# A message-passing GNN on one core: pairs of groups and a deeper ring in the two sums, one signal fewer in the two maxima

## The chip, the core and the metric

One NeuronCore of a Trainium2 chip runs the whole program. TensorE (PE) multiplies into PSUM, VectorE (DVE) and ScalarE (ACT) read PSUM, GpSimd (POOL) issues indirect DMAs that gather rows, SyncE (SP) issues plain DMAs. The engines wait for each other through semaphores, counters that an instruction raises when it is done. The metric is the device time of one execution in microseconds (us); lower is better.

## The reference

There are 12500 nodes with 96 features and 200000 edges sorted by destination. Four rounds pass over all the edges:

```
h  = relu(layernorm(x))
n1 = mean over edges of h[src];   n2 = mean over edges of n1[src]
x  = x + 0.5 * n1 + 0.5 * n2                      # rounds 0 and 1: sums
h  = relu(layernorm(x))
c1 = leaky(max over edges of (h[src] @ W1_msg + edge_attr @ W1_edge) + h @ W1_root + b1)
c2 = leaky(max over edges of (c1[src] @ W2_msg + edge_attr @ W2_edge) + c1 @ W2_root + b2)
out = x + c2                                      # rounds 2 and 3: maxima
```

A node without edges gets 0. All is float32; the inputs are drawn at random.

## The kernel before

The edges are cut into batches of 128, one edge a partition, and four batches make a group: 391 groups, 1564 batches. Each round has an edge phase (all groups) and a node phase (14 chunks of seven tiles of 128 nodes), and a table in HBM holds the values that the round gathers from. The phases of a round follow each other; the change touches the edge phases alone.

*Gather (all rounds).* GpSimd runs a stream written out in full: for each group four indirect DMAs (L374), each 128 rows of 384 bytes into one slot of a ring `rows` of `RING` = 8 groups. Before a group from the ninth on it waits until the group that had the slot is used: for `picked` in the sums, for `rows_ps` in the maxima, both raised by TensorE.

*Sums (rounds 0 and 1).* In a batch the edges of one node are neighbours. VectorE builds for each group four one-hot matrices from the edge's rank within its batch's window (`hots`, L767; L773 in round 0 builds a second set for counting the nodes of each tile), two groups ahead. TensorE (`sum_windows`) multiplies each batch's rows by its one-hot (L557, four matmuls of two records each) into one of two PSUM banks (`WIN + j % 2 * BANK`), raises `picked`, and in round 0 multiplies ones by the counting one-hots (L563), raising `counted`. It starts a group when the rows have landed, the one-hots are there and the fold two groups back is done. VectorE's `fold` (L784) waits for `picked`, loads four start positions into registers and adds four windows into `comp`, one after another. In round 0 ScalarE writes a column of node numbers into each ring slot (`stage_ids`, L435).

*Maxima (rounds 2 and 3).* TensorE's order within a step g is: `rows_of(g)` (edge features times weights, L576, and the rows by identity, L578; raises `rows_ps`), `back(g-1)` (transposes the running maxima, L589; raises `runT_ps`), `pick(g-2)` (one-hots pick the last of each segment, L600; raises `picked`). VectorE scans each group (L799) and builds its one-hots; ScalarE copies the transposes to SBUF (`copy_running`, L443) and the picked windows into `comp` (`windows`, L452).

`sweeps` runs a body of eight groups: once written out, then in a loop, then the rest. VectorE, ScalarE and TensorE use it; GpSimd's stream has no loop. Waits are in each engine's program order; nothing is reordered.

## Time and profile before

| | us |
|---|---|
| median of 3 runs | 9666.22 |
| lowest, highest | 9662.51, 9667.9 |
| the profiled execution | 9629.93 |
| its span, first to last instruction | 9628.2 |
| GpSimd busy | 6458.6 (67%) |
| TensorE busy | 5576.1 (58%) |
| VectorE busy | 3262.5 (34%) |
| ScalarE busy | 1500.7 (16%) |

The profile is one execution, recorded by the hardware. "Idle before" is the time an engine did nothing before an instruction, and the arrow names what ended it: "issue" is nothing that the profile shows, "remote" a semaphore update whose origin it does not show. The granted clock of TensorE has two levels, 0.5 (1.2 GHz) and 1.0 (2.4 GHz). Matmul ends are modelled. Round 0's edge phase is about 60 to 2331 us, round 1's 2412 to 4666, round 2's 4776 to 7113, round 3's 7212 to 9550.

### The profile page before, as it was taken

The page shows a single profiled execution, that of the slowest core. Times are in us where ns is not written, and L with a number is a line of the kernel's source. Part 1 is how long each engine was busy: PE and PEld are TensorE (multiplying, and loading weights), DVE is VectorE, ACT ScalarE, POOL GpSimd, SP SyncE. Part 2 cuts the span into 40 slices and gives each one's busy share as a digit, 9 for nine tenths or more (in the row PEclk, how much of TensorE's full clock was granted, in tenths as well). Part 3 has the DMA queues.
Part 4 walks back from the last instruction along what each step waited for, and adds up shares of the span by engine and source line. Part 5 has one row for each costly group of instructions (what it writes and reads, how often), then busy time and mean ns, then how long its engine had stood idle before and what let it go on. Part 6 is the DMA issues. An engine that isn't in the chain of part 4 may idle for free.

```text
span 9628.2 us, 100471 instructions
## 1 busy us (share of the span) xinstructions
PE 5576.1 (58%) x25651; PEld 4095.6 (43%) x25651; DVE 3262.5 (34%) x6693; ACT 1500.7 (16%) x5073; POOL 6458.6 (67%) x6525
## 2 busy tenths in 40 slices
PE   2333333334233333333578877878887887887888
PEld 1222222223222222222555555555564555555556
DVE  4333333334333232323423333333332333333334
ACT  1000000001000000000322222222232222222223
POOL 5666666664666666666566666766656666666665
PEclk6555555556555555555767777777786777677776
DMA  3111111111111111111133333333323333333332
GB/s 79 35 34 34 34 34 34 34 35 39 47 35 34 34 34 35 34 34 35 46 76 77 77 77 77 78 80 78 77 64 71 80 78 77 77 77 77 77 81 64
DMA packets 309643, 548.56 MB, mean 57 GB/s; under 512 B 183464, under 2 KB 183464, under 8 KB 284712
## 3 DMA queue, kind: packets, MB, share of 16 engines
q0 software_dynamic: 200192, 307.90, 16.3%
q1 hardware_dynamic: 108804, 239.50, 9.7%
q14 instruction: 77, 0.63, 0.0%
q8 instruction: 22, 0.36, 0.0%
q10 hardware_dynamic: 548, 0.17, 0.0%
HBM read 522.27 MB, written 24.87 MB: 57 GB/s over the span
## 4 chain that ended last, share of the span: by engine, by line
another core or an unknown queue 29%; PE 26%; issue 9%; DVE 8%; DVEq 2%; ACT 1%; ACTq 1%; POOL 0%; DMA 0%; POOLq 0%; SPq 0%
PE ps L578 7%; PE ps L576 6%; PE ps L600 6%; PE ps L589 3%; DVE arena L799 3%; DVE comp L784 3%; PE ps L557 2%; DVE arena L767 2%; DVEq L257 1%; DVEq L784 1%; PE ps L662 1%; PE ps L638 0%; ACTq L257 0%; PE ps L675 0%
## 5 line engine op out<-in xcount | busy, mean ns | idle before, releaser
L374 POOL DMA_INDIRECT rows<-table,src_sb x6256 | 6273.4, 1003 | 2930.3 <-issue 1767.5
L557 PE MATMUL ps<-arena,rows 128*98 128x128 f32 (+1 forms) x6256 | 1418.1, 399 | 2967.0 <-DVE comp L784 2634.6
L557 PEld LDWEIGHTS ps<-arena,rows 128*98 128x98 f32 (+1 forms) x6256 | 1179.5, 254 | 3226.7 <-DVE comp L784 2836.3
L799 DVE TENSOR_TENSOR_SCAN arena<-arena,ps 96x512 f32<-96x512 f32 x782 | 996.6, 1274 | 3238.6 <-remote 1989.8
L784 DVE TENSOR_TENSOR comp<-comp,ps 98x128 f32 (+1 forms) x3128 | 893.6, 286 | 2878.4 <-remote 2317.0
L578 PEld LDWEIGHTS ps<-ident,rows 128*96 128x96 f32 x6256 | 950.4, 208 | 912.9 <-issue 912.7
L600 PE MATMUL ps<-arena 128*96 128x128 f32 x6256 | 1180.2, 352 | 108.6 <-issue 72.4
L578 PE MATMUL ps<-ident,rows 128*96 128x128 f32 x6256 | 1173.3, 344 | 54.2 <-issue 53.4
L576 PE MATMUL ps<-arena,we 32*96 32x512 f32 x1564 | 1143.7, 819 | 27.3 <-DMA rows<-table,src_sb 27.3
L600 PEld LDWEIGHTS ps<-arena 128*96 128x96 f32 x6256 | 1052.2, 228 | 129.6 <-issue 124.4
L767 DVE TENSOR_TENSOR arena<-iota_b,meta 128x512 f32<-128x512 bf16 x1564 | 1053.0, 673 | 59.6 <-issue 55.1
L452 ACT COPY comp<-ps 96x128 f32 x3128 | 821.3, 263 | 1490.8 <-PE ps L600 573.6
L589 PE MATMUL ps<-ident,arena 96*128 96x96 f32 x3128 | 564.2, 322 | 757.8 <-DVE arena L799 653.8
L589 PEld LDWEIGHTS ps<-ident,arena 96*128 96x128 f32 x3128 | 449.1, 190 | 831.0 <-DVE arena L799 657.9
L443 ACT COPY arena<-ps 128x384 f32<-128x384 f32 x782 | 374.5, 479 | 1998.1 <-remote 1233.2
L435 ACT COPY rows<-root 128x4 f32 (+1 forms) x391 | 74.3, 197 | 2179.0 <-remote 1581.1
L492 ACT COPY rel_c<-node_rel 128x7 f32<-128x7 f32 (+1 forms) x42 | 8.5, 203 | 2261.8 <-DVE comp L784 2261.8
L388 POOL TENSOR_SCALAR arena<-iota,rel_c 128x128 f32<-128x128 f32 x252 | 172.0, 698 | 228.4 <-ACT rel_c L492 134.0
L576 PEld LDWEIGHTS ps<-arena,we 32*96 32x96 f32 x1564 | 236.2, 196 | 186.9 <-issue 125.4
L773 DVE TENSOR_TENSOR arena<-iota_b,meta 128x392 bf16<-128x392 bf16 x391 | 219.5, 561 | 12.0 <-issue 11.6
L563 PE MATMUL ps<-arena,ones_b 128*1 128x392 bf16 x391 | 168.3, 430 | 0.0
L662 PE MATMUL ps<-arena 128*128 128x96 f32 (+1 forms) x784 | 141.1, 354 | 6.4 <-ACT arena L504 4.8
(84 smaller groups left out, 1026.0 us busy)
## 6 DMA issues: line engine op xcount, KB each, us to landing
arena<-flags SPq DMA_DIRECT2D x194, 768.0 KB
rows<-table,src_sb POOLq DMA_INDIRECT x6256
arena<-in_eat SPq DMA_DIRECT2D x194, 256.0 KB
table<-arena SPq DMA_DIRECT2D x56, 336.0 KB, 2.7
out<-xs SPq DMA_DIRECT2D x13, 336.0 KB
xs<-in_x SPq DMA_DIRECT2D x6, 672.0 KB, 5.9
arena<-flags SPq DMA_DIRECT2D x2, 576.0 KB
src_sb<-in_srcs SPq DMA_DIRECT2D x1, 782.0 KB, 5.2
```

Source lines behind the costliest of these rows:

```text
L374: pool.indirect_dma_start(rows[:, g % RING, j, 0:D], None, tables[r][:, :], bass.IndirectOffsetOnAxis(src_sb[:, c:c + 1], 0)).then_inc(lan ...
L443: act.copy(runT[:, slot % SCANS].rearrange("p k d -> p (k d)"), ps[:, RUNT + slot % 2 * BANK:RUNT + slot % 2 * BANK + GRP * D]).then_inc(r ...
L452: act.copy(comp[0:D, bass.ds(at, P)], ps[0:D, WIN + slot % 2 * BANK + j * P:WIN + slot % 2 * BANK + (j + 1) * P]).then_inc(folded[r], 1)
L557: m = pe.matmul(ps[0:w, at + k * P:at + (k + 1) * P], rows[:, j, k, 0:w], hot[:, j % HOTS, k, :], start=True, stop=True)
L576: pe.matmul(ps[0:D, at:at + W], we[D:P, r - 2, :], fe[D:P, u, q * W:(q + 1) * W], start=True, stop=False)
L578: m = pe.matmul(ps[0:D, at + k * P:at + (k + 1) * P], rows[:, slot, k, 0:D], ident[:, :], start=False, stop=(k == GRP - 1))
L589: m = pe.transpose(ps[:, at:at + D], run[:, slot % SCANS, k * P:(k + 1) * P], ident[0:D, 0:D])
L600: m = pe.matmul(ps[0:D, at:at + P], runT[:, slot % SCANS, k, :], hot[:, slot % HOTS, k, :], start=True, stop=True)
L662: m = pe.matmul(ps[:, at_spread + j * P:at_spread + j * P + w], spread_c[:, qs, j, :], win_c[:, qs, j, 0:w], start=True, stop=True)
L767: dve.tensor_tensor(hot[:, slot % HOTS], ids, rel, ALU.is_equal).then_inc(hot_ready[r], 1)
L784: dve.tensor_tensor(win, win, ps[0:w, of:of + P], ALU.add).then_inc(folded[r], 1)
L799: dve.tensor_tensor_scan(run[:, slot % SCANS], fe[0:D, slot // UNIT, q * W:(q + 1) * W], ps[0:D, ROWS + slot % 2 * BANK:ROWS + slot % 2 * ...
```

## The change

In the sums the ring has `DEEP` = 16 slots; the eight new ones (`rows_x`) lie in the arena behind the one-hots, which get eight slots instead of four. TensorE works by `PAIR` = 2 groups: it waits once for the one-hots, node numbers and fold of the pair, does the count matmul of a group ahead of its four matmuls, and raises `picked` once, after the second group. The windows have four PSUM banks instead of two, and a pair starts when the fold two pairs back is done. `counted` is gone. VectorE builds one-hots six groups ahead (`AHEAD`) and folds by pairs. GpSimd and ScalarE wait for pairs. The loop body `turns` has sixteen groups. In round 1 the new slots may be written only when round 0's node phase is over. In the maxima `back` and `pick` raise one semaphore, `turned`, after the pick, where they raised two; `rows_ps` stays. The diff, cut to its core:

```diff
 RING = 8
+DEEP = 16
+PAIR = 2
+AHEAD = 6
...
-        tile_hot, at2 = carve(at, [P, HOTS, GRP, TILES], BF16)
+        hot_s, at2 = carve(0, [P, 2 * HOTS, GRP, P])
+        tile_hot, at2 = carve(at2, [P, 2 * HOTS, GRP, TILES], BF16)
+        rows_x, at2 = carve(at2, [P, DEEP - RING, GRP, X])
...
-        WIN, ROWS, RUNT, COUNT = 0, 2 * BANK, 6 * BANK, 2 * BANK
+        WIN, ROWS, RUNT, COUNT = 0, 2 * BANK, 6 * BANK, 4 * BANK
...
+        def turns(engine, body):
+
+            body(0, DEEP)
+            with engine.Fori(1, TURNS - 1) as i:
+                body(i, DEEP)
+            body(TURNS - 1, REST)
+
+        def ring(k):
+
+            return rows[:, k] if k < RING else rows_x[:, k - RING]
+
+        def landings_before(r, k):
+
+            return 16 * GRP * r * len(range(k, GROUPS, DEEP))
...
-                used = picked[r] if r in sums else rows_ps[r]
+                deep = DEEP if r in sums else RING
                 for g in range(GROUPS):
-                    if g >= RING:
-                        pool.wait_ge(used, g - RING + 1)
+                    if r == 1 and g == RING:
+                        pool.wait_ge(stepA[0], CHUNKS * STEPS[0])
+                    if g >= deep:
+                        if r in sums:
+                            pool.wait_ge(picked[r], (g - DEEP) // PAIR + 1)
+                        else:
+                            pool.wait_ge(rows_ps[r], g - RING + 1)
                     for j in range(GRP):
                         c = g * GRP + j
-                        pool.indirect_dma_start(rows[:, g % RING, j, 0:D], None, tables[r][:, :],
+                        pool.indirect_dma_start(ring(g % deep)[:, j, 0:D], None, tables[r][:, :],
                                                 bass.IndirectOffsetOnAxis(src_sb[:, c:c + 1], 0)
-                                                ).then_inc(landed[r][g % RING], 16)
+                                                ).then_inc(landed[r][g % deep], 16)
...
-                        g = i * RING + j
-                        if after(i, 1):
-                            act.wait_ge(picked[0], g - (RING - 1))
-                        act.copy(rows[:, j, :, D + 1], node1[:, bass.ds(i * (RING * GRP) + j * GRP, GRP)]
+                        if after(i, 1) and j % PAIR == 0:
+                            act.wait_ge(picked[0], i * (DEEP // PAIR) + (j // PAIR + 1 - DEEP // PAIR))
+                        act.copy(ring(j)[:, :, D + 1], node1[:, bass.ds(i * (DEEP * GRP) + j * GRP, GRP)]
                                  ).then_inc(ids_ready, 1)
...
-                    act.wait_ge(runT_ps[r], g + 1)
+                    act.wait_ge(turned[r], g + 1)
                     if after(g, SCANS):
-                        act.wait_ge(picked[r], g - (SCANS - 1))
+                        act.wait_ge(turned[r], g - (SCANS - 2))
                     act.copy(runT[:, slot % SCANS].rearrange("p k d -> p (k d)"),
                              ps[:, RUNT + slot % 2 * BANK:RUNT + slot % 2 * BANK + GRP * D]).then_inc(runT_sb[r], 1)
...
-                    act.wait_ge(picked[r], g + 1)
+                    act.wait_ge(turned[r], g + 2)
...
                 def sum_windows(i, n):
 
                     w = X if r == 0 else D
-                    for j in range(n):
-                        g = i * RING + j
-                        pe.wait_ge(hot_ready[r], g + 1)
+                    for first in range(0, n, PAIR):
+                        both = range(first, min(first + PAIR, n))
+                        pair = i * (DEEP // PAIR) + first // PAIR
+                        done = i * DEEP + (both[-1] + 1)
+                        pe.wait_ge(hot_ready[r], done)
                         if r == 0:
-                            pe.wait_ge(ids_ready, g + 1)
-                        pe.wait_ge(landed[r][j], i * (16 * GRP) + 16 * GRP)
-                        if after(g, 2):
-                            pe.wait_ge(folded[r], g * GRP - GRP)
-                        at = WIN + j % 2 * BANK
-                        for k in range(GRP):
-                            m = pe.matmul(ps[0:w, at + k * P:at + (k + 1) * P], rows[:, j, k, 0:w], hot[:, j % HOTS, k, :],
-                                          start=True, stop=True)
+                            pe.wait_ge(ids_ready, done)
+                            pe.wait_ge(tile_ready, done)
+                        if after(pair, 2):
+                            pe.wait_ge(folded[r], pair * (PAIR * GRP) - PAIR * GRP)
+                        for j in both:
+                            pe.wait_ge(landed[r][j], i * (16 * GRP) + (16 * GRP + landings_before(r, j)))
+                            if r == 0:
+                                pe.matmul(ps[0:1, COUNT:COUNT + GRP * TILES], ones_b[:, :],
+                                          tile_hot[:, j % (2 * HOTS)].rearrange("p k t -> p (k t)"),
+                                          start=(known(i) and i == 0 and j == 0),
+                                          stop=(known(i) and i * DEEP + j == GROUPS - 1), skip_group_check=True)
+                            at = WIN + j % (2 * PAIR) * BANK
+                            for k in range(GRP):
+                                m = pe.matmul(ps[0:w, at + k * P:at + (k + 1) * P], ring(j)[:, k, 0:w],
+                                              hot_s[:, j % (2 * HOTS), k, :], start=True, stop=True)
                         m.then_inc(picked[r], 1)
-                        if r == 0:
-                            pe.wait_ge(tile_ready, g + 1)
-                            last = known(g) and g == GROUPS - 1
-                            pe.matmul(ps[0:1, COUNT:COUNT + GRP * TILES], ones_b[:, :],
-                                      tile_hot[:, j % HOTS].rearrange("p k t -> p (k t)"),
-                                      start=(known(g) and g == 0), stop=last, skip_group_check=True).then_inc(counted, 1)
...
-                    m.then_inc(runT_ps[r], 1)
+                    return m
...
-                    m.then_inc(picked[r], 1)
+                    return m
 
                 def max_windows(i, n):
 
@@ -607,20 +640,23 @@
                         g = i * RING + j
                         rows_of(i, g, j)
                         if after(g, 1):
-                            back(g - 1, j - 1)
-                        if after(g, 2):
-                            pick(g - 2, j - 2)
+                            m = back(g - 1, j - 1)
+                            if after(g, 2):
+                                m = pick(g - 2, j - 2)
+                            m.then_inc(turned[r], 1)
...
-                    pick(GROUPS - 1, LAST - 1)
+                    pick(GROUPS - 2, LAST - 2).then_inc(turned[r], 1)
+                    pick(GROUPS - 1, LAST - 1).then_inc(turned[r], 1)
...
-            step(dve.memset(rows[:, :, :, D], 1.0))
...
-                        dve.wait_ge(picked[r], g - (HOTS - 1))
+                        dve.wait_ge(turned[r], g - (HOTS - 2))
+                    rel = meta[:, 2, bass.ds(g * GRP, GRP)].unsqueeze(2).to_broadcast([P, GRP, P])
...
+                def sum_hots(g, slot):
+
+                    at = bass.ds(g * GRP, GRP)
+                    rel = meta[:, 0, at].unsqueeze(2).to_broadcast([P, GRP, P])
+                    ids = iota_b[:, :].unsqueeze(1).to_broadcast([P, GRP, P])
+                    dve.tensor_tensor(hot_s[:, slot % (2 * HOTS)], ids, rel, ALU.is_equal).then_inc(hot_ready[r], 1)
                     if r == 0:
-                        if after(g, HOTS):
-                            dve.wait_ge(counted, g - (HOTS - 1))
                         tile = meta[:, 1, at].unsqueeze(2).to_broadcast([P, GRP, TILES])
                         ids = iota_b[:, 0:TILES].unsqueeze(1).to_broadcast([P, GRP, TILES])
-                        dve.tensor_tensor(tile_hot[:, slot % HOTS], ids, tile, ALU.is_equal).then_inc(tile_ready, 1)
+                        dve.tensor_tensor(tile_hot[:, slot % (2 * HOTS)], ids, tile, ALU.is_equal).then_inc(tile_ready, 1)
...
-                    dve.wait_ge(picked[r], g + 1)
-                        of = WIN + slot % 2 * BANK + j * P
+                        of = WIN + slot % (2 * PAIR) * BANK + j * P
                         dve.tensor_tensor(win, win, ps[0:w, of:of + P], ALU.add).then_inc(folded[r], 1)
...
-                        dve.wait_ge(runT_ps[r], g - (SCANS - 1))
+                        dve.wait_ge(turned[r], g - (SCANS - 1))
...
                 def add_windows(i, n):
 
-                    for j in range(n):
-                        g = i * RING + j
-                        if not (known(g) and g + 2 >= GROUPS):
-                            hots(g + 2, j + 2)
-                        fold(g, j)
+                    for first in range(0, n, PAIR):
+                        pair = i * (DEEP // PAIR) + first // PAIR
+                        if after(pair, 1):
+                            dve.wait_ge(picked[r], pair)
+                        for j in range(first + AHEAD, first + AHEAD + PAIR):
+                            if not (known(i) and i * DEEP + j >= GROUPS):
+                                sum_hots(i * DEEP + j, j)
+                        dve.wait_ge(picked[r], pair + 1)
+                        for j in range(first, min(first + PAIR, n)):
+                            fold(i * DEEP + j, j)
...
+                if r == 0:
+                    dve.memset(rows[:, :, :, D], 1.0).then_inc(ones_set, 1)
+                    dve.memset(rows_x[:, :, :, D], 1.0).then_inc(ones_set, 1)
                 if r in sums:
-                    hots(0, 0)
-                    hots(1, 1)
+                    for g in range(AHEAD):
+                        sum_hots(g, g)
...
-                sweeps(dve, add_windows if r in sums else run_maxima)
+                if r in sums:
+                    turns(dve, add_windows)
+                else:
+                    sweeps(dve, run_maxima)
...
-                    dve.wait_ge(counted, GROUPS)
+                    dve.wait_ge(picked[0], PAIRS)
```

## Rows read from the trace of the kernel before

**Rows 1.** The page's busy times: us (share of the span) x instructions

```profile
PE 5576.1 (58%) x25651; PEld 4095.6 (43%) x25651; DVE 3262.5 (34%) x6693; ACT 1500.7 (16%) x5073; POOL 6458.6 (67%) x6525
```

**Rows 2.** The page's costliest group: count | busy us, mean ns | idle before

```profile
L374 POOL DMA_INDIRECT rows<-table,src_sb x6256 | 6273.4, 1003 | 2930.3 <-issue 1767.5
```

**Rows 3.** GpSimd's waits (total us, times, longest), rounds 0, 1, 2, 3

```profile
POOL rows L374 <- issue: 448.3, 1470, 0.4
POOL rows L374 <- remote: 269.0, 90, 4.3
...
POOL rows L374 <- remote: 253.9, 82, 5.8
...
POOL rows L374 <- remote: 246.9, 126, 2.8
POOL rows L374 <- PE ps L578: 24.9, 15, 6.1
...
POOL rows L374 <- remote: 238.5, 124, 3.0
POOL rows L374 <- PE ps L578: 36.6, 23, 6.5
```

**Rows 4.** Timeline of round 0: start, us, what [idle before]

```profile
979.25 0.94 POOL L374 DMA_INDIRECT rows<-table,src_sb  x1 [3.22 <-remote]
980.50 0.95 POOL L374 DMA_INDIRECT rows<-table,src_sb  x1 [0.30 <-issue]
...
986.72 1.69 PE L557 MATMUL ps<-arena,rows 128*98 128x128 f32 x8
...
989.25 1.12 PE L557 MATMUL ps<-arena,rows 128*98 128x128 f32 x8 [0.59 <-DVE comp L784]
...
995.86 0.20 ACT L435 COPY rows<-root 128x4 f32 x1 [9.35 <-remote]
...
996.47 1.55 DVE L784 TENSOR_TENSOR comp<-comp,ps 98x128 f32 x4 [5.92 <-remote]
...
997.93 0.68 DVE L767 TENSOR_TENSOR arena<-iota_b,meta 128x512 f32<-128x512 bf16 x1
...
998.07 2.02 PE L557 MATMUL ps<-arena,rows 128*98 128x128 f32 x8 [7.44 <-DVE comp L784]
998.53 0.56 DVE L773 TENSOR_TENSOR arena<-iota_b,meta 128x392 bf16<-128x392 bf16 x1
...
1000.02 0.48 PE L563 MATMUL ps<-arena,ones_b 128*1 128x392 bf16 x1
...
1003.97 0.94 POOL L374 DMA_INDIRECT rows<-table,src_sb  x1 [0.30 <-issue]
1007.89 0.37 ACT L435 COPY rows<-root 128x4 f32 x2 [11.83 <-remote]
1008.04 0.94 POOL L374 DMA_INDIRECT rows<-table,src_sb  x1 [3.13 <-remote]
1008.39 1.55 DVE L784 TENSOR_TENSOR comp<-comp,ps 98x128 f32 x4 [9.29 <-remote]
...
1009.99 2.02 PE L557 MATMUL ps<-arena,rows 128*98 128x128 f32 x8 [9.49 <-DVE comp L784]
```

**Rows 5.** Groups on GpSimd, first 185 us; then 2412 to 2505 us

```profile
L374 POOL DMA_INDIRECT rows<-table,src_sb x86 | 92.4, 1075 | 79.4 <-DMA table<-arena 46.9 <-issue 25.3 <-remote 7.2
...
L374 POOL DMA_INDIRECT rows<-table,src_sb x66 | 65.3, 989 | 34.9 <-issue 19.2 <-remote 8.4 <-DMA table<-arena 7.3
```

**Rows 6.** Timeline, last gather and last fold of rounds 0 and 1

```profile
2314.54 0.95 POOL L374 DMA_INDIRECT rows<-table,src_sb  x1 [0.30 <-issue]
...
2329.57 1.55 DVE L784 TENSOR_TENSOR comp<-comp,ps 98x128 f32 x4 [0.24 <-DVE comp L784]
...
4651.46 0.95 POOL L374 DMA_INDIRECT rows<-table,src_sb  x1 [0.30 <-issue]
...
4664.06 1.53 DVE L784 TENSOR_TENSOR comp<-comp,ps 96x128 f32 x4 [0.24 <-DVE comp L784]
```

**Rows 7.** Groups of TensorE in round 2 (4776 to 7212 us)

```profile
L600 PE MATMUL ps<-arena 128*96 128x128 f32 x3128 | 590.1, 352 | 52.7 <-issue 41.3 <-ACT arena L443 11.1
L578 PE MATMUL ps<-ident,rows 128*96 128x128 f32 x3128 | 586.6, 344 | 25.9 <-issue 25.6
...
L589 PE MATMUL ps<-ident,arena 96*128 96x96 f32 x1564 | 281.0, 321 | 382.1 <-DVE arena L799 338.4 <-issue 42.8
```

27 lines of the change are left out of this document (16 added, 11 removed).

## The prediction

> **What bounds the kernel now.** I read the page's busy shares first. GpSimd is the busiest engine at 67% [rows 1], nearly all of it one line, the indirect gather L374: 6256 of them, 1003 ns each, with 2930 us of idle time around them [rows 2]. So the next view is GpSimd's waits round by round [rows 3]. "issue" is the 0.3 us between two gathers and never goes away (448.3 us over 1470 gaps in round 0). The wait that can go is "remote", together with the few put down to TensorE: 269.0, 253.9, 271.8 (246.9 + 24.9) and 275.1 us (238.5 + 36.6), 1070 us in all, 11% of the span. The code says what it is: the ring of eight groups is full and GpSimd waits for TensorE's signal that a group is used. A gather costs 0.95 + 0.30 us [rows 4], a group of four 5.0 us; 391 groups take 1955 us; at the mean of 1003 ns [rows 2] 2038 us.
>
> The reader would now suspect TensorE or VectorE of being too slow. The timeline says otherwise [rows 4]. Per group TensorE works 2.02 us at the 0.5 clock and 1.12 us at full clock, plus 0.48 us for the count; VectorE works 1.55 + 0.68 + 0.56 = 2.8 us. Both are far under 5.0 us. What is late is the signal. Number the folds: the one at 996.47 adds the group that TensorE ran at 986.72, the one at 1008.39 the group run at 989.25, because the matmul at 1009.99 may start only when the fold two groups back is done, and one group (998.07) lies between. So results written by about 988.4 and 990.4 are seen at 995.9 and 1007.9: 7 and 17 us late. Three engines wake within 0.5 us of each other (ScalarE 1007.89, GpSimd 1008.04, VectorE 1008.39), with TensorE silent since about 1000.5. That means the count itself arrived then. "remote" is the name of a release whose update the trace lacks. And it arrives 3 us after GpSimd's last gather (1003.97 + 0.94 = 1004.91) and not before. I read this as: while gathers are issued without a break, TensorE's signals get stuck, and they come through when GpSimd falls quiet. The pattern is periodic: GpSimd resumes at 979.25 and again at 1008.04, 20 gathers (five groups) apart, and pays 3.13 us each time.
>
> This does not happen from the first gather. Of the first 86 gathers of round 0 the ring wait took 7.2 us in two waits, and of the first 66 of round 1 8.4 us in two [rows 5]: 0.33 and 0.51 us a group, against 269.0/391 = 0.69 and 253.9/391 = 0.65 over the rounds.
>
> **The change part by part.** The sum is made against the profiled execution, 9629.9 us (span 9628.2). The median of the runs is 9666.2, 36 us more; I add the change in time to the median.
>
> *Four banks, pairs, ring of sixteen (rounds 0 and 1).* A cycle is a stretch of gathers and one stall. Today it feeds GpSimd five groups: two whose signals come with the quiet moment (two banks, so TensorE is two groups ahead of the folds), then two or three whose signals still pass. After the change two pairs, four groups, come with the quiet moment, giving 20 us of gathers. The third pair: fold of a pair 2 x 1.55 plus its address loads, about 3.6 us, then eight matmuls 4.0 us, signal at about 8 us, which still passes today (the groups after 1008.04). The fourth and fifth pairs are served late, by 7 and 17 us as in rows 4, but inside the 40 us by then bought. So ten to twelve groups a stall where there were five. The stall also gets longer with the stretch: 3.1 to 3.2 us after 20 gathers [rows 4], two waits of together 7.2 and 8.4 us in the starts of 86 and 66 gathers [rows 5]. Bounds for the stall per group after: 0 (all signals in time: one per pair, 10 us) and 0.69 (nothing helps: the share is the same in all four rounds, whatever their number of signals). The nearest rows are the two starts, the only long stretches: (7.2 + 8.4)/(152/4) = 0.41 us. They begin from a quiet GpSimd, so I take 0.50. Sum: 782 x 0.50 = 391 against 522.9: **-132 us**. Bounds -523 and +17 (782 x 0.69 = 540).
>
> The count matmul's own signal goes with it (391 signals). Round 1 has one signal a group, round 0 two, and the ring waits differ by 15 us only: a signal fewer a group and round is worth 15 us. In the sums this is inside the term above.
>
> *The price of the deeper ring.* A round isn't over when the last gather lands: what lies in the ring is still to be added. Round 0: gathers end at 2314.54 + 0.95, the last fold ends at 2331.12, 15.6 us for seven groups; round 1: 4652.41 to 4665.59, 13.2 us for six and a bit [rows 6]. That is 2.2 and 2.1 us a group. With sixteen slots full there are up to eight groups more: 17.8 + 16.9 = **+35 us**; nothing where the ring isn't full. Between them I take 35, since stalls mean a full ring.
>
> *One-time parts.* Six one-hots instead of two before round 0: 4 x (0.68 + 0.56) = 5 us on VectorE, and two memsets of some 0.1 us; GpSimd gathers meanwhile and has sixteen free slots. Cost 0, 5 us if the first fold set the end of the first ring. Round 1's wait for round 0's node phase at the ninth group comes 40 us after the gathers start, long satisfied: 0. Six one-hots ahead in steady state change nothing in VectorE's work. Instruction streams: loop bodies of sixteen groups instead of eight; no row shows a fetch stall, bound 0 to 1 us per turn, 24 turns and two rounds, 48 us; I take 0, because the loops of today show only the 0.3 us gaps.
>
> *Two of three signals become one (rounds 2 and 3).* In each step TensorE feeds the scan (its own signal), transposes group g-1 and picks g-2. Now the transposes are announced only after the picks: ScalarE's copy of g-1 starts later by the pick, four matmuls of two records, 8 x 0.352 = at most 2.8 us by the records and 2.02 or 1.1 us in sequence. Behind ScalarE's wait is its own window copy, which needed the pick anyway. The copy (0.48 us) is wanted at the pick of the next step, after the rows (8 x 0.344) and a transposition (4 x 0.321) [rows 7], over 3 us at either clock with the edge matmuls: it fits. Gain: one signal fewer a group, 15 us a round by the comparison above, bounds 0 and, if all three signals cost alike, a third of 547 = 182 us. Taken: **-30 us**. GpSimd's own release, the rows' signal, stays.
>
> The Trainium skill has a rule on increments ("TensorE: Matmul & The Clock Gate", The cost: per-tile semaphore tail): increments on matmuls queue one behind another, about 26 ns each. The change takes away 391 + 195 + 195 in the sums (one count signal and half or more of the others) and 782 in the maxima, 1563; by that rule alone this is 41 us, and only where it is on the path. The lateness of 7 and 17 us in rows 4 is several hundred times what it gives, so the trace doesn't agree that this is all that a signal costs.
>
> Sum: -132 + 35 - 30 = -127 us. 9629.9 - 127 = 9503; on the median 9666 - 127 = 9539. I say **9535**.
>
> **The rivals.**
> *A, the stalls nearly vanish.* If what is served late is one signal per so many microseconds, then pairs halve the demand to one in 10 us, and a slack of sixteen groups covers 17 us of lateness. For it: at the starts 20 groups pass with two waits. Against: they do stall, with most signals of isolated groups. Sums -523 x 0.8 = -418, no tail, maxima up to -100: about 9150 to 9300.
> *B, the stall keeps its share.* Rounds 0 to 3 spend 269, 254, 272 and 275 us in it although their signals per group are two, one, three and three. If that is a law of GpSimd's issue (so much quiet per gather), nothing in the signals or the ring matters. Then 0 for the stalls, perhaps the tail: 9666 to 9700.
> *C, slower.* The merged signal. It stands behind the pick, and the pick waits for ScalarE's earlier copy. Where the signals are stuck, the copy's release is now one place later in TensorE's order; once the cover of over 3 us is used up, every ring stall of rounds 2 and 3 (126 + 15 + 124 + 23 = 288 waits) grows by one pick, 1.1 to 2.0 us: 288 x 1.5 = +430, against -97 in the sums: 10000. It decides from the point where the copy is later than TensorE's next rows. With half of the stalls, 9785. Against it: TensorE's idle time before the picks is now 41 + 11 us of a round [rows 7].
> *D, the change doesn't do what it says*: VectorE's fold waits for the first of two pairs anyway and the banks are never four deep. Then only tail and -30: about 9670, with B.
>
> **How the numbers follow.** Forecast (half-cured stalls, 9400 to 9645) 0.50; A (below 9400) 0.25; B and D 0.15, of which 0.12 are within 0.2% (19 us, what this kernel's measurement can tell from no change) and 0.03 above; C 0.10. Faster 0.75, same 0.12, slower 0.13. The likeliest is 9535. For 8 in 10 the range reaches into A to 9260 and into B to 9660; the forecast alone would be 9400 to 9645.
>
> **What would show it.** Right: in rounds 0 and 1 GpSimd's ring wait at about 0.5 us a group, 390 us in both, in waits 40 to 60 us apart instead of 25 to 29; folds still 5 us or more behind TensorE's matmuls; more groups added after the last gather, some 15 with 30 us. Rounds 2 and 3: ring wait 240 to 275 us, idle time before the picks not above 52 us. A shows as ring waits under 100 us in both sums. B shows as waits of 250 us or more in each with longer stalls further apart. C shows as idle time of TensorE before L600's matmuls released by ScalarE's copy. The prediction is wrong if the sums' ring wait doesn't fall, or falls below 200, or if the maxima move by more than 100 us.

## The result, and the profile after

The changed kernel takes 9719.05 us (median of 4 runs, 9701.79 to 9724.75) against 9664.36 us for the kernel before measured beside it (9656.97 to 9667.9): ratio 1.0054, 95% interval 1.0039 to 1.0070. It is slower by half a per cent. The profiled execution took 9701.79 us (span 9700.1), 71.9 us more than the one before. The medians differ by 54.7 us, so some 17 of the 71.9 are the spread between single executions.

The page after, the busy times and the groups that answer to [rows 1, 2]. The gather has two rows, because half of the slots now lie in the arena:

```profile
PE 5429.9 (56%) x25651; PEld 4047.2 (42%) x25651; DVE 3296.0 (34%) x6694; ACT 1487.5 (15%) x5073; POOL 6478.4 (67%) x6525
...
L404 POOL DMA_INDIRECT rows<-table,src_sb x4720 | 4781.1, 1013 | 2269.1 <-issue 1334.3
...
L404 POOL DMA_INDIRECT arena<-table,src_sb x1536 | 1513.3, 985 | 686.3 <-issue 449.2
...
L633 PE MATMUL ps<-arena 128*96 128x128 f32 x6256 | 1164.6, 348 | 509.4 <-issue 322.8
```

The gathers are 21.0 us longer in sum (4781.1 + 1513.3 against 6273.4) and the idle time before them is 25 us more. (The picks of TensorE, L633, are for the maxima below.) The waits by round say where. GpSimd's waits of the changed kernel, rounds 0 and 1, then 2 and 3 (us in total, times, longest), against [rows 3]:

```profile
POOL rows L404 <- remote: 83.1, 24, 13.8
POOL arena L404 <- remote: 79.0, 19, 5.4
...
POOL rows L404 <- PE ps L596: 42.8, 10, 5.1
POOL arena L404 <- PE ps L596: 18.2, 4, 5.2
...
POOL arena L404 <- remote: 139.9, 39, 12.8
POOL rows L404 <- remote: 118.6, 34, 6.5
...
POOL rows L404 <- remote: 244.0, 111, 6.6
POOL rows L404 <- PE ps L611: 56.2, 45, 2.6
...
POOL rows L404 <- remote: 239.9, 108, 3.9
POOL rows L404 <- PE ps L611: 53.0, 36, 2.4
```

Sums: 223.1 + 258.5 = 481.6 us where there were 522.9. Maxima: 300.2 + 292.9 = 593 us where there were 547. The ring works as built, but the stalls are only rarer and longer: in the two sums 130 waits with a mean of 3.7 us and a longest of 13.8 us, where there were 172 with a mean of 3.0 and a longest of 5.8. A stall now comes every 6.0 groups instead of every 4.5.

With each round's edge phase cut at its first and last gather in the trace, the 71.9 us are all placed. The last row runs to the last fold; in rounds 2 and 3, which have no folds, to ScalarE's last window copy.

| us, before / after | round 0 | round 1 | round 2 | round 3 |
|---|---|---|---|---|
| first gather to last | 2254.5 / 2261.6 | 2239.5 / 2242.0 | 2309.0 / 2328.7 | 2309.3 / 2323.0 |
| of it, gathers busy | 1536.3 / 1579.5 | 1533.8 / 1526.6 | 1602.1 / 1595.4 | 1601.2 / 1592.9 |
| of it, gaps over 0.5 us | 265.6 / 222.5 | 253.9 / 261.4 | 271.2 / 305.7 | 273.9 / 298.4 |
| last gather to last fold or copy | 15.6 / 30.3 | 13.2 / 28.1 | 26.7 / 26.7 | 27.2 / 28.3 |

Sums: +9.6 in the gathering and +29.6 behind it. Maxima: +33.4 and +1.1. Everything between them: -2. In round 0 the ring wait did fall, by 43 us, and the gathers got longer by 43 us.

What a stall looks like now. Timeline of the changed kernel in round 0 (start, us, what, count, idle before):

```profile
999.73 1.55 DVE L822 TENSOR_TENSOR comp<-comp,ps 98x128 f32 x4 [11.35 <-remote]
...
1001.62 0.29 DVE L822 TENSOR_TENSOR comp<-comp,ps 98x128 f32 x1 [0.33 <-issue]
...
1004.09 0.29 DVE L822 TENSOR_TENSOR comp<-comp,ps 98x128 f32 x1 [2.18 <-issue]
...
1008.24 0.94 POOL L404 DMA_INDIRECT rows<-table,src_sb  x1 [0.30 <-issue]
1009.00 0.29 DVE L822 TENSOR_TENSOR comp<-comp,ps 98x128 f32 x1 [2.50 <-issue]
...
1009.35 0.49 PE L590 MATMUL ps<-arena,ones_b 128*1 128x392 bf16 x1 [20.55 <-issue]
...
1014.31 1.04 POOL L404 DMA_INDIRECT rows<-table,src_sb  x1 [5.13 <-PE ps L596]
...
1024.73 0.68 DVE L808 TENSOR_TENSOR arena<-iota_b,meta 128x512 f32<-128x512 bf16 x1
1024.81 1.89 POOL L404 DMA_INDIRECT rows<-table,src_sb  x1 [0.30 <-issue]
...
1025.33 0.56 DVE L812 TENSOR_TENSOR arena<-iota_b,meta 128x392 bf16<-128x392 bf16 x1
```

Two things. First, while GpSimd gathers, the others crawl: TensorE idles 20.55 us, and VectorE's folds, whose starts are some 0.4 us apart otherwise, come 2.1 to 2.8 us apart, though no wait on TensorE stands between them. Once GpSimd stops (at 1009.18), the pair is through in 5 us. Second, at 1024.81 a gather that starts beside the builds of one-hots (L808, L812) takes 1.89 us, twice the usual 0.94.

The tail, for [rows 6]: last gather and last folds of rounds 0 and 1 of the changed kernel.

```profile
2322.75 0.94 POOL L404 DMA_INDIRECT rows<-table,src_sb  x1 [0.30 <-issue]
...
2352.88 1.13 DVE L822 TENSOR_TENSOR comp<-comp,ps 98x128 f32 x3 [0.24 <-DVE comp L822]
...
4673.40 0.94 POOL L404 DMA_INDIRECT rows<-table,src_sb  x1 [0.30 <-issue]
...
4701.77 0.70 DVE L822 TENSOR_TENSOR comp<-comp,ps 96x128 f32 x2 [0.23 <-DVE comp L822]
```

And TensorE in round 2, for [rows 7]:

```profile
L633 PE MATMUL ps<-arena 128*96 128x128 f32 x3128 | 588.8, 351 | 285.2 <-issue 190.7 <-ACT arena L472 94.4
...
L622 PE MATMUL ps<-ident,arena 96*128 96x96 f32 x1564 | 268.0, 310 | 211.8 <-DVE arena L837 162.1 <-issue 49.4
```

TensorE now stands 285 us ahead of its picks where it stood 53.

### The profile page after: what moved, and what is told of

Read it like the earlier page. It is cut to its first block, busy times and chain, and to the rows that moved or that the text cites. A ratio compares the mean times of both kernels' runs of the same rounds, so it can differ in the third digit from the quotient of the medians.

```text
span 9700.1 us, 99108 instructions
## 1 busy us (share of the span) xinstructions
PE 5429.9 (56%) x25651; PEld 4047.2 (42%) x25651; DVE 3296.0 (34%) x6694; ACT 1487.5 (15%) x5073; POOL 6478.4 (67%) x6525
## 4 chain that ended last, share of the span: by engine, by line
PE 27%; another core or an unknown queue 13%; issue 7%; DVE 2%; ACT 1%; ACTq 1%; DVEq 0%; POOL 0%; DMA 0%; POOLq 0%; SPq 0%
PE ps L633 8%; PE ps L611 8%; PE ps L609 7%; PE ps L622 3%; DVE arena L837 2%; PE ps L698 1%; ACT comp L481 0%; PE ps L711 0%; ACTq L282 0%; PE ps L674 0%; DVE arena L801 0%; ACT arena L514 0%; ACT arena L472 0%; ACT arena L449 0%
## 5 line engine op out<-in xcount | busy, mean ns | idle before, releaser
L404 POOL DMA_INDIRECT rows<-table,src_sb x4720 | 4781.1, 1013 | 2269.1 <-issue 1334.3
L404 POOL DMA_INDIRECT arena<-table,src_sb x1536 | 1513.3, 985 | 686.3 <-issue 449.2
L633 PE MATMUL ps<-arena 128*96 128x128 f32 x6256 | 1164.6, 348 | 509.4 <-issue 322.8
L633 PEld LDWEIGHTS ps<-arena 128*96 128x96 f32 x6256 | 1032.4, 224 | 538.7 <-issue 499.2
L609 PE MATMUL ps<-arena,we 32*96 32x512 f32 x1564 | 1141.6, 818 | 26.7 <-DMA rows<-table,src_sb 26.7
L596 PE MATMUL ps<-arena 128*98 128x128 f32 (+1 forms) x3072 | 656.6, 390 | 873.6 <-DVE comp L822 748.8
L596 PE MATMUL ps<-arena,rows 128*98 128x128 f32 (+1 forms) x3184 | 691.3, 395 | 780.8 <-DVE comp L822 591.9
L596 PEld LDWEIGHTS ps<-arena 128*98 128x98 f32 (+1 forms) x3072 | 569.2, 251 | 950.0 <-DVE comp L822 756.4
L596 PEld LDWEIGHTS ps<-arena,rows 128*98 128x98 f32 (+1 forms) x3184 | 600.4, 255 | 870.8 <-DVE comp L822 493.0
L622 PE MATMUL ps<-ident,arena 96*128 96x96 f32 x3128 | 538.3, 311 | 511.2 <-DVE arena L837 423.8
L590 PEld LDWEIGHTS ps<-arena,ones_b 128*1 128x1 bf16 x391 | 30.9, 79 | 1540.6 <-DVE comp L822 877.6
L808 DVE TENSOR_TENSOR arena<-iota_b,meta 128x512 f32<-128x512 bf16 x782 | 526.0, 687 | 219.5 <-issue 210.8
```

The lines of the kernel that those rows point to most:

```text
L404: pool.indirect_dma_start(ring(g % deep)[:, j, 0:D], None, tables[r][:, :], bass.IndirectOffsetOnAxis(src_sb[:, c:c + 1], 0)).then_inc(lan ...
L596: m = pe.matmul(ps[0:w, at + k * P:at + (k + 1) * P], ring(j)[:, k, 0:w], hot_s[:, j % (2 * HOTS), k, :], start=True, stop=True)
L609: pe.matmul(ps[0:D, at:at + W], we[D:P, r - 2, :], fe[D:P, u, q * W:(q + 1) * W], start=True, stop=False)
L622: m = pe.transpose(ps[:, at:at + D], run[:, slot % SCANS, k * P:(k + 1) * P], ident[0:D, 0:D])
L633: m = pe.matmul(ps[0:D, at:at + P], runT[:, slot % SCANS, k, :], hot[:, slot % HOTS, k, :], start=True, stop=True)
L808: dve.tensor_tensor(hot_s[:, slot % (2 * HOTS)], ids, rel, ALU.is_equal).then_inc(hot_ready[r], 1)
```

## The experiments: which part costs

Four kernels on one chip, five rounds each, against the kernel before at 9548.97 us there. "Gathering" is the time from the first gather of a round to its last, "tail" the time from there to the last fold, both from the one profiled execution of each.

**The sums alone** (the maxima's two signals as before) and **the maxima alone** (the merged signal in the kernel before).

```diff
 # e1, from the changed kernel            # e2, from the kernel before
+ m.then_inc(runT_ps[r], 1)    (back)     - m.then_inc(runT_ps[r], 1)    (back)
+ m.then_inc(picked[r], 1)     (pick)     - m.then_inc(picked[r], 1)     (pick)
- m.then_inc(turned[r], 1)                + m.then_inc(turned[r], 1)     (behind the pick)
```

> The change in the sums alone; the maxima signal as before. Theory Q (quiet): a stuck signal of TensorE comes through only after GpSimd has been quiet for a time that grows with the stretch of gathers before it, some 1.4 us + 0.1 us a gather, so the ring wait is a share of the gathers and hardly a matter of ring, banks or number of signals. Then the sums are as in the changed kernel (ring wait 222 and 261 us, last folds 30 us after the last gather) and the maxima as before (ring wait 270 to 275 us each): 33 us faster than the changed kernel, 0.2 to 0.4% slower than before. Theory S (signals cost each): three signals a group in the maxima are worse than two, so this is slower than the changed kernel.

> The merged signal in the maxima alone; the sums as before. Theory L (the announcement of the transposes is late by a pick, and ScalarE's copy with it): ring wait in the maxima 300 us each as in the changed kernel, TensorE's idle time before the picks of L600's kind about 250 us a round instead of 53; 30 to 35 us slower than before. Theory S (signals cost each): faster than before by 15 us or more.

e1: 9578.51 us, ratio 1.0033 [1.0021, 1.0046]. e2: 9576.38 us, ratio 1.0030 [1.0020, 1.0040]. Both parts cost, about 30 and 27 us, and together they are the whole. In e1 the gathering of rounds 0 and 1 takes 2237.2 and 2221.2 us, in e2, whose sums are the old ones, 2235.3 and 2219.9: ring, banks and pairs move it by 2 us. The rest of e1's loss is the tail (32.1 + 27.5 against 15.5 + 18.0). The gathering of rounds 2 and 3 takes 2294.7 and 2297.3 in e2, 2284.0 and 2285.2 in e1: +23 us for the two rounds by the merged signal. The ring waits missed what was expected in microseconds, because on this chip all are shorter (e1: 189 and 228 us in the sums for 222 and 261; e2: 273 and 278 us in the maxima for 300), but the differences between the kernels came as expected.

**Pairs with the ring of eight, and the ring of sixteen without pairs.**

```diff
-DEEP = 16          # e3          -PAIR = 2          # e4
+DEEP = 8                         +PAIR = 1
```

> As e1_sums_only with a ring of eight slots instead of sixteen (pairs, four banks, one signal a pair stay; eight groups a loop body). Theory Q: the stretches between stalls are bought by signals and not by slots, so ring wait as in e1 or up to 0.05 us a group more, and the tails after the last gather are 15 us a round shorter: as before the change or up to 20 us faster. Rival: the depth is what kept the ring wait down, and with four pairs only the wait rises above 300 us a round: 50 us slower or more.

> As e1_sums_only with pairs of one: ring of sixteen, but signals and folds by group and two banks. Theory Q with the two-bank cycle: stretches of 20 gathers again, ring wait 250 to 270 us a round, tails 30 us: 30 to 40 us slower than before. Rival (depth pays by itself): ring wait under 200 us a round and faster than before.

e3: 9545.65 us, ratio 0.9993 [0.9984, 1.0002]. e4: 9582.30 us, ratio 1.0033 [1.0021, 1.0045]. The deeper ring alone carries the loss of the sums (tails of 38.1 and 33.4 us in e4, 19.0 and 17.0 in e3), pairs alone do nothing that can be measured. The gathering of round 0 takes 2234.8 us in e3 and 2233.7 in e4, in each of the four kernels within 4 us. But its parts differ: gathers 1589.4 and gaps 184.6 us in e3, 1537.8 and 242.0 in e4. The sum is 1774 and 1780. What the waits lose comes back in the gathers.

## The experiments: what the stall is

Four kernels on a second chip (before 9640.3 us), one profiled run each, the last also timed in three rounds.

**GpSimd never waits for TensorE.** In the sums it waits for its own landings of eight groups earlier; TensorE reads fixed slots.

```diff
-                    if g >= deep:
+                    if g >= RING:
-                            pool.wait_ge(picked[r], (g - DEEP) // PAIR + 1)
+                            pool.wait_ge(landed[r][(g - RING) % DEEP], ...)
-                        pool.indirect_dma_start(ring(g % deep)[:, j, 0:D], ...
+                        pool.indirect_dma_start(rows[:, g % RING, j, 0:D], ...
```

> The sums alone as in the changed kernel, but in the two sum rounds TensorE reads eight fixed slots (all ones) that no gather writes, and GpSimd gathers into the eight slots of the ring before and waits for its own landings of eight groups earlier, never for TensorE. The output is not the reference's. Late signals (TensorE's signals reach GpSimd late while it gathers, and the ring waits are the price): the waits of 190 and 228 us in the stage of gathers of rounds 0 and 1 go, the stages fall from 2237 and 2221 us to 2050 and 1990 us, and the whole to about 9150 us on a chip where the kernel before takes 9549. Own pace (the gathers and their queue take 5.7 us a group whoever releases the slots; where a gather runs longer a wait is shorter by as much): the stages stay within 20 us of 2237 and 2221 us.

10963.04 us. The gathering falls only to 2175.9 and 2164.0 us, and behind it come 826.5 and 683.5 us in which TensorE and VectorE do what they had not done. The gather group of this kernel in round 0, VectorE's waits in the window from 1000 to 2000 us, and a timeline over two pairs:

```profile
L406 POOL DMA_INDIRECT rows<-table,src_sb x1564 | 1679.3, 1074 | 542.7 <-issue 496.6 <-DMA table<-arena 46.1
```

```profile
DVE comp L823 <- remote: 796.2, 20, 40.7
```

```profile
982.82 0.49 PE L592 MATMUL ps<-arena,ones_b 128*1 128x392 bf16 x1 [41.29 <-DVE comp L823]
...
992.24 0.37 PE L598 MATMUL ps<-arena 128*98 128x128 f32 x1 [2.53 <-issue]
...
1028.56 1.56 DVE L823 TENSOR_TENSOR comp<-comp,ps 98x128 f32 x4 [39.92 <-remote]
...
1033.22 0.49 PE L592 MATMUL ps<-arena,ones_b 128*1 128x392 bf16 x1 [40.61 <-DVE comp L823]
...
1042.64 0.37 PE L598 MATMUL ps<-arena 128*98 128x128 f32 x1 [2.53 <-issue]
...
1078.96 0.72 DVE L823 TENSOR_TENSOR comp<-comp,ps 98x128 f32 x2 [39.92 <-remote]
```

TensorE starts a pair when the pair two back is folded: the matmul at 1033.22 follows the folds that began at 1028.56. So the fold at 1078.96 adds the pair that ran from 982.82 to 992.6, and VectorE hears of it 86 us late (the pair that ends at 1043 is folded at 1129). A pair takes 50.4 us in round 0 (44.8 in round 1) while GpSimd gathers, and 5.5 (4.5) us after its last gather. TensorE also stops for 2.2 to 2.8 us, twice in each pair, before a matmul that waits for nothing (992.24, 1042.64). Nor are the gathers free: from start to start they run in spells of 1.25 us and of 1.40 us, these with nothing of VectorE beside them:

```profile
900.93 1.00 POOL L406 DMA_INDIRECT rows<-table,src_sb  x1 [0.30 <-issue]
902.24 1.09 POOL L406 DMA_INDIRECT rows<-table,src_sb  x1 [0.30 <-issue]
903.64 1.09 POOL L406 DMA_INDIRECT rows<-table,src_sb  x1 [0.30 <-issue]
...
914.54 0.95 POOL L406 DMA_INDIRECT rows<-table,src_sb  x1 [0.30 <-issue]
915.79 0.94 POOL L406 DMA_INDIRECT rows<-table,src_sb  x1 [0.30 <-issue]
```

Both theories are half right. The signals are late only while GpSimd gathers, and the quiet in the ring wait is what lets the sums get on. But with no wait at all the gathering is only 79 and 76 us shorter than in the trace before (78 and 76 than in e8 below, which has the old sums on this same chip): by this one execution that, and not 523 us, was all that the waits of the sums could give.

**Half of each row.** As many descriptors, 192 bytes each.

```diff
-                        pool.indirect_dma_start(ring(g % deep)[:, j, 0:D], None, tables[r][:, :],
+                        pool.indirect_dma_start(ring(g % deep)[:, j, 0:HALF[r]], None, tables[r].rearrange("n (h d) -> (n h) d", d=HALF[r]),
```

> The sums alone as in the changed kernel, but each gather of the two sum rounds fetches 48 columns of a row in place of 96, as many descriptors of half the bytes; the output is not the reference's. Late signals: nothing in the wait hangs on bytes, the stages of gathers stay at 2237 and 2221 us within 15. Own pace, if it is one of bytes: the ring waits of 190 and 228 us shrink by at least a third (stages 2175 and 2145 us or less).

9663.32 us; gathering 2257.3 and 2235.4 us, gaps 212.5 and 255.3. The gathering is 20 and 14 us over what was expected from the other chip, and within 5 us of the old sums on this one (2254.1 and 2239.9 in e8). Half the bytes save nothing.

**No one-hots of windows** behind the first eight groups.

```diff
+                    if not known(g) or g >= 2 * HOTS:
+                        dve.memset(spare[:, 0, slot % (2 * HOTS)], 0.0).then_inc(hot_ready[r], 1)
```

> The sums alone as in the changed kernel, but VectorE builds the one-hots of windows for the first eight groups of a round only, and signals after a write of one column for each later group (the one-hots of tiles in round 0 stay); the output is not the reference's. Do longer gathers come out of the ring waits? The gathers that ran beside VectorE's builds (round 1: mean 980 ns against 950 for the others) get shorter in round 1, to 950 to 965 ns, 25 to 45 us in the stage. Conserved: the ring waits of round 1 grow by as much, and its stage stays at 2221 us within 8. Independent: the stage of round 1 falls by 25 to 45 us.

9647.6 us. GpSimd's groups of this kernel in round 1:

```profile
L405 POOL DMA_INDIRECT rows<-table,src_sb x796 | 753.2, 946 | 385.5 <-issue 232.8 <-remote 144.1 <-DMA table<-arena 8.6
L405 POOL DMA_INDIRECT arena<-table,src_sb x768 | 724.4, 943 | 378.1 <-issue 224.6 <-remote 153.5
```

The gathers are 945 ns, 51 us less in the round than with half rows on the same chip, and the ring waits are 297.6 us, 42 more. The gathering: 2232.7 against 2235.4. The sum is conserved, as the second theory had it.

**TensorE picks before it transposes,** three signals kept.

```diff
-                        if after(g, 1):
-                            back(g - 1, j - 1)
                         if after(g, 2):
                             pick(g - 2, j - 2)
+                        if after(g, 1):
+                            back(g - 1, j - 1)
```

> The kernel before, with one change in the maxima: TensorE makes the windows of the group two back first and transposes the running maxima of the last group behind them, all three signals kept. So ScalarE is told of a transposed group as late as with the one common signal. Late copy (the common signal costs because the copy of the running maxima starts behind the windows): the stages of gathers of rounds 2 and 3 are 10 to 16 us longer than with the order before (2284 us there), ratio 1.002 to 1.003. Something in the joint wait itself (VectorE's one-hots and ScalarE's second wait, which the common signal also moved): the stages stay at 2284 within 4 us, ratio 1.000.

9680.3 us, ratio 1.0041 [1.0027, 1.0055]. The gathering of rounds 2 and 3 takes 2334.3 and 2328.3 us; the three kernels with the old maxima on this chip have 2307.3 to 2310.5. That is 18 to 27 us a round, more than the 10 to 16 expected of a late copy. But this order does more than make the copy late: the pick now stands ahead of the next transposition too, so ScalarE has that much less time for its copy. TensorE's group of picks in both maxima of e2, then of e8, for [rows 7]:

```profile
L600 PE MATMUL ps<-arena 128*96 128x128 f32 x6256 | 1170.1, 349 | 641.2 <-issue 439.4 <-ACT arena L443 201.3
```

```profile
L600 PE MATMUL ps<-arena 128*96 128x128 f32 x6256 | 1197.5, 355 | 1072.3 <-ACT arena L443 624.6 <-issue 446.8
```

TensorE waits 201 us for the copy with the merged signal and 625 us with the pick first. So lateness alone, with all three signals kept, can cost more than the merged signal did. That the joint wait has a share in e2's 27 us isn't excluded, and the saved signal gained nothing that shows.

## The experiments: sessions without the stall

These runs come from three more sessions, on three chips (e9 to e11, e12 to e15, e16 to e18).

**A fourth of the windows, each window twice, and bf16 windows,** to tell late signals from matmuls that are themselves held up step by step.

```diff
-                            for k in range(GRP):
+                            for k in range(GRP if known(i) and i == 0 else 1):    # e9, e12
+                            for k in [*range(GRP), *range(GRP)]:                  # e10, e13
-   pe.matmul(ps[0:w, ...], ring(j)[:, k, 0:w], hot_s[:, j % (2 * HOTS), k, :], ...)
+   pe.matmul(ps[0:w, ...], ones_w[:, 0:w], hot_b[:, j % (2 * HOTS), k, :], ...)      # e11, e14
```

> The sums alone as in the changed kernel, but behind the first sixteen groups of a sum round TensorE makes the first of a group's four windows only (same waits, same signals, VectorE adds what stands in PSUM); the output is not the reference's. With GpSimd never waiting, a pair of groups took 50.4 us in round 0 and 44.8 us in round 1, exactly 36 and 32 gathers of 1.40 us: 4 gathers for each of the 8 matmuls, 2 more for each of the two counting ones. Two theories. Steps: TensorE's matmuls themselves get on while GpSimd gathers by a step per gather (4 steps a matmul), and what is left over is made up in the ring wait; then a fourth of the matmuls leaves almost no ring wait in round 1 (228 us before to under 60) and its stage falls from 2235 to 2000-2080 us on this chip. Signals: only the signals are late, one per pair as before; then the ring waits stay at 200 us or more and the stage within 30 us of 2235.

> The sums alone as in the changed kernel, but TensorE makes each window of the sum rounds twice into the same PSUM place, with no more signals. Steps: the stage of gathers of a sum round holds 280 us (2235 less 1564 gathers at 1.25 us) for TensorE's 1564 matmuls, in ring waits and in longer gathers; twice the matmuls adds 200 to 300 us a round, the whole goes up by 400 to 600 us. Signals: TensorE is busy 0.4 us in 1.43 us of a gather and can hide the second set; the stages grow by less than 60 us.

> The sums alone as in the changed kernel, but the windows' matmuls take bf16 one-hots and a fixed bf16 weight of ones in place of float32 one-hots and rows: as many matmuls and signals, each matmul in one pass where float32 takes four (0.373 us down to about 0.1 us); the output is not the reference's. Steps by passes: a fourth of the steps, so the ring waits of round 1 fall under 60 us and its stage from 2235 to 2000-2080 us, as with a fourth of the matmuls. Steps by matmul: nothing in their number has changed, stage within 30 us of 2235. Signals: likewise within 30 us of 2235.

8655.51, 8621.52 and 8609.51 us, where the kernel before took 8536.05, and not one ring wait over 0.5 us. These runs tell nothing of the two theories, since what the theories explain didn't occur. They ran again on another chip, with the kernel before for its trace:

> One of four windows again, for a chip that shows the ring waits (one where the kernel before takes over 9500 us; where it takes 8536 us GpSimd never waited for the ring, and the run before told nothing of the two theories). The output is not the reference's. Steps: ring wait of round 1 under 60 us, its stage 2000-2080 us. Signals: ring waits of 200 us or more, stage within 30 us of 2235.

> Each window of the sums made twice, again for a chip that shows the ring waits. Steps: the stages of rounds 0 and 1 grow by 200 to 300 us each. Signals: they grow by less than 60 us.

> As many matmuls and signals as in the sums alone, in bf16 with a fixed weight, again for a chip that shows the ring waits; the output is not the reference's. Steps by passes: ring wait of round 1 under 60 us, stage 2000-2080 us. Steps by matmul, or signals: stage within 30 us of 2235.

> The kernel before, for its own trace on this chip. If it is a chip with ring waits: about 265, 255, 270 and 270 us of them in the four rounds, gathers of 0.98 us in the sums and 1.02 us in the maxima. If it is one without: no ring waits, stages of gathers of 1995 to 2030 us.

8658.11, 8647.17 and 8628.64 us, the kernel before 8523.32 (8526.12 beside them), again without such waits. But this was the chip of e1 to e4, where the same kernel had taken 9548.97 less than an hour earlier. So the stall is a matter of the session and not of the chip, and what brings it is not known. GpSimd's group of e15 in 60 to 2200 us, then in 2170 to 4320 us (the windows take in some gathers of the next round); its idle time holds no wait for TensorE:

```profile
L374 POOL DMA_INDIRECT rows<-table,src_sb x1582 | 1570.7, 993 | 534.9 <-issue 481.5 <-DMA table<-arena 53.4
...
L374 POOL DMA_INDIRECT rows<-table,src_sb x1606 | 1537.5, 957 | 516.1 <-issue 488.8 <-DMA table<-arena 27.3
```

**The changed kernel in such a session (e16 to e18), and both kernels with one operand of the one-hots in float32.**

```diff
-                    ids = iota_b[:, :].unsqueeze(1).to_broadcast([P, GRP, P])
+                    ids = iota_0[:, :].unsqueeze(1).to_broadcast([P, GRP, P])
```

> The changed kernel itself, because in the last two sessions the chips ran the kernel before in 8526 to 8536 us with no ring wait in its trace. If that is met again there is nothing in the sums for a deeper ring to save: the forecast's term is zero and what is left is its cost. Gathers beside VectorE's one-hots: the pair's two or four builds in a row hold up gathers, the gather stages of rounds 0 and 1 are 65 to 100 and 25 to 40 us longer than 2027 and 1973 us, the whole 8620 to 8660, ratio 1.010 to 1.016. No such effect: 8526 to 8545, ratio 1.000 to 1.002. If it is a chip with ring waits again (before over 9500): ratio 1.004 to 1.007 as first measured.

> The kernel before, with one operand of VectorE's one-hots (the row of numbers) read as float32 in place of bf16; the values are the same. In every trace only those gathers took over 0.95 us that overlapped these builds (512 float32 from bf16, 0.675 us; 392 bf16 from bf16, 0.57 us), none that overlapped the folds or the scans, which read float32. Hold by 16-bit operands: gathers of all rounds fall to 0.945-0.955 us; without ring waits the whole gets 150 to 250 us shorter (8300 to 8380, ratio 0.970 to 0.982), with ring waits less than 60 us, since the waits take up what the gathers save. Hold by the broadcast or by the size of the output: gathers stay at 0.96 to 0.99 us, ratio 0.998 to 1.003.

> The changed kernel with the same one operand read as float32. Hold by 16-bit operands, and the builds being the whole cost of the change in the sums: its gathers fall to 0.945-0.955 us too and it stands within 0.5% of the kernel before with that operand (tails of 15 us longer a sum round are left). Hold by something else: it stays where the changed kernel is.

e16: 8674.15 us against 8520.61, ratio 1.0180 [1.0166, 1.0194]. e17: 8521.8, ratio 1.0002 [0.9993, 1.0011]. e18: 8675.03, ratio 1.0179 [1.0165, 1.0193]. The operand's type does nothing; that theory fell. The loss is larger than I had expected, and it lies where expected: the gathering takes 2130.9 and 2013.5 us in rounds 0 and 1 where e15 has 2027.4 and 1972.8 (+103.5, +40.7), with a difference of at most 5 us in rounds 2 and 3. Against e17, the old sums on the same chip, it is +107.2 and +39.3. Behind the last gather e16 needs 7.3 and 6.9 us and e15 6.8 and 6.7: where the ring isn't full, the deeper one has no tail. And TensorE stands 1 us in all before the picks of round 2: where signals are in time, the merged one costs nothing. The timeline of e16 in round 0:

```profile
1004.78 0.69 DVE L808 TENSOR_TENSOR arena<-iota_b,meta 128x512 f32<-128x512 bf16 x1
1005.38 0.56 DVE L812 TENSOR_TENSOR arena<-iota_b,meta 128x392 bf16<-128x392 bf16 x1
1005.86 0.69 DVE L808 TENSOR_TENSOR arena<-iota_b,meta 128x512 f32<-128x512 bf16 x1
1005.86 1.98 POOL L404 DMA_INDIRECT arena<-table,src_sb  x1 [0.30 <-issue]
1006.46 0.56 DVE L812 TENSOR_TENSOR arena<-iota_b,meta 128x392 bf16<-128x392 bf16 x1
1008.14 0.94 POOL L404 DMA_INDIRECT arena<-table,src_sb  x1 [0.31 <-issue]
```

and of the kernel before in the same kind of session (e15):

```profile
1003.33 0.68 DVE L767 TENSOR_TENSOR arena<-iota_b,meta 128x512 f32<-128x512 bf16 x1
1003.93 0.56 DVE L773 TENSOR_TENSOR arena<-iota_b,meta 128x392 bf16<-128x392 bf16 x1
1003.99 1.32 POOL L374 DMA_INDIRECT rows<-table,src_sb  x1 [0.30 <-issue]
1005.61 0.94 POOL L374 DMA_INDIRECT rows<-table,src_sb  x1 [0.30 <-issue]
```

A gather caught by builds ends about 0.8 us behind the last build of the run (7.84 against 7.02, 5.31 against 4.49). The pair puts four builds in a row where there were two, so the hold grows from 1.3 to 2 us (a few near the start of the changed kernel's round 0 reach 3.1); in both traces all but a few of the gathers over 1.1 us overlapped builds, and those that overlapped none took 0.94 us in both. That the order of the builds is the cause is read from these overlaps; no run in such a session changes the order alone. Here GpSimd is the bound, and this goes straight into the time. With the stall, it goes into the waits.

## Why the prediction was wrong

The forecast was 9535 us, faster than before; measured were 9719.05 us, slower. Rival B named the outcome in the sums ("the stall keeps its share ... perhaps the tail: 9666 to 9700"), and C the sign in the maxima.

- **The ring term, -132, failed.** It was read as a price per stall, to be spread over more groups. The measured wait is 481.6/782 = 0.62 us a group, not 0.50, so -41 us instead of -132; and of these 41 the gathers took back 36 (1579.5 + 1526.6 against 1536.3 + 1533.8). The gaps that are no longer waits cost their usual 0.30 us, 9 us more, so the gathering came out 10 us longer. The step that failed is "a stretch of gathers and one stall", with "ten to twelve groups a stall where there were five": it was 6.0 for 4.5, each stall was longer, and waits and lengths of gathers are one account. e1 to e4 show it (round 0 within 4 us with rings of 8 and 16, groups and pairs), e7 from the other side, and e5 the ceiling of 154 us. Why it is one account is not known. The bounds held the value; the nearest rows that I chose, the starts [rows 5], were the wrong ones, since they begin without a debt.
- **"0 when nothing helps" was the right reading of four equal rounds.** That rounds with one, two and three signals a group pay 254 to 275 us [rows 3] was the strongest row against the forecast, and I gave it 0.15.
- **The tail, +35, was right:** +14.7 and +14.9, and it comes with the ring of sixteen (32.1 + 27.5 in e1 and 19.0 + 17.0 in e3, which differ in the depth alone).
- **The one-time parts, 0, were right** within 2 us. But "six one-hots ahead in steady state change nothing in VectorE's work" missed that their order changed: four builds in a row hold up a gather. With the stall it cost nothing that can be told apart; without it, the longer gathers of the two sums are 144 of the 154 us.
- **The merged signal, -30, failed in sign:** +34.5 us in the trace, +27 by e2. The cover of "over 3 us" is there only while signals are in time: TensorE's idle time before the picks of round 2 rose from 53 to 285 us here, and is 1 us in e16. C had the mechanism, and its size of 430 or 215 us was wrong: a late copy doesn't lengthen each of 288 stalls by a pick. A price of 15 us a signal, from rounds that differ in more than signals, was no price. The Trainium skill ("TensorE: Matmul & The Clock Gate", The cost: per-tile semaphore tail) has about 26 ns an increment for tiles that run side by side in the array. By that rule the 781 increments that e3 drops would be an estimated 20 us; its ratio of 0.9993 [0.9984, 1.0002] doesn't show them.

What stays open: what in the chip delays TensorE's signals while GpSimd gathers, whether its matmuls are held up or only their news, and why it does so in one session and not in another. More than news is held up: in round 0 of e5 TensorE stops 80 times for over 1 us before a window's matmul that waits for nothing, and in round 0 of the changed kernel VectorE does so 123 times before a fold; in round 0 of e15 and e16 neither does it once. With GpSimd never waiting, a pair takes 36 gathers in round 0 and 32 in round 1, of 1.40 us in the mean. That could be four for each float32 matmul and two for each bf16 one; e9 to e14 were to test that as steps, and met no stall. No version is measurably faster than the kernel before.

## What to carry to other kernels

When an engine waits for a slot and the wait is the same share whatever the number of signals, first run it with no wait at all: what the waiting stage gains then is the ceiling of a deeper buffer. Look at the waiting engine's own instructions too, since a wait that shrinks can come back as longer instructions. And when groups are processed in pairs, the order on a third engine changes as well: here the kernel with two short runs of builds on VectorE had shorter gathers than the one with a long run.

## What the runs showed of the hardware

- In some sessions TensorE's signals reach all engines late while GpSimd issues indirect DMAs without a break: 7 and 17 us in [rows 4], where they come when it pauses, and 86 us in e5, where it doesn't pause. The landings of the gathers are not late: in 2000 gathers each of the traces before and after, of e5 and of e15 the last packet ends 1.2 us after the gather in the median, and under 1.35 us in 99 of 100. In another session on the same chip as e1 to e4 ScalarE starts 0.12 us after TensorE's last matmul ends, and the whole is about 1000 us shorter (8526 against 9549).
- An indirect DMA of 128 rows costs GpSimd 0.94 us and 0.30 us between two; half the bytes cost the same. Beside builds of one-hots it mostly takes up to 2 us (3.1 at most), beside folds (98x128, float32) 0.94 us. e5 is an exception that isn't explained, and that e17's expectation ("in every trace") passes over: there it also takes 1.09 us with nothing beside it, and over 1.1 us beside folds.
- Making each window twice cost nothing that single executions show in a session without the stall (8621.52 us against 8609.51 for bf16 and 8655.51 for a fourth of them): there TensorE is off the path.
